# Other tables for the order in which four engines interleave a selective scan with an FFN, on one core

## Chip, cores and metric

The kernel runs on one core of a Trainium2 chip. The metric is the device time in microseconds. A core has four compute engines that run beside one another, each in the order of its own program: TensorE (PE, with its weight loads as PEld), VectorE (DVE), ScalarE (ACT) and GpSimd (POOL). SyncE (SP) issues most of the DMAs. The engines wait for one another only by semaphores.

## What is computed

For a batch of 4 sequences of 256 tokens with 256 features, a mixer and an FFN are added one after the other:

```python
x = x + xattn(ctx, layernorm(x))      # selective scan, gated by silu(layernorm(x))
x = x + ffn(layernorm(x))
# xattn: u = silu(causal_conv4(in_proj(ctx)) + b);  dt_low, B, C = split(x_proj(u))
#        dt = softplus(dt_proj(dt_low) + b);  A = -exp(A_log), 16 states per channel
#        state = state * exp(dt * A) + (dt * u) * B;   y = sum_n state * C + D * u;   out = y * silu(z)
# ffn:   h = layer_norm(gelu(silu(bitlinear(x, w1, b1)))) ;  bitlinear(h, w2, b2)      (256 -> 1024 -> 256)
# bitlinear: rms norm, activations quantised to 8 bits by row, weights to -1, 0, 1 by their mean
```

## The kernel before

**Mixer.** The recurrence over time is done by VectorE's scan instruction. The work is cut into 32 units, `where(k)`: batch b = k // 8, half h of the 256 channels, group of 4 of the 16 states. A unit is 128 channels by 4 x 256 columns. It passes through the engines in this order:

- ScalarE, `exps(k)`: four exponentials give exp(dt * A) into a ring of 6 buffers (L692). It waits for scan k - 6.
- TensorE, `scale_b(k)` and `scale_rest(k)`: 8 small matmuls each (L512) give dt * u * B into one of two PSUM slots. scale_b(k) waits for scan k - 2.
- VectorE, `scan(k)`: L1006, into a ring of 4 buffers. It waits for sum k - 4.
- GpSimd, `prod(k)`: the state times C (L847), for which a DMA has spread C over the partitions.
- TensorE, `sum_states(k)`: 8 transposing matmuls (L551) add the states up in PSUM; a unit that begins a half also adds D * u (L545).

Each batch needs, ahead of its units, small steps: `convolve` (L451), `silu_u` (L658), `xdbl` (L462), `copy_xd` (L664), `dtraw` (L480), `dt_bias` (L672), `dt_neg` (L950), `dt_exp` (L678, L680), `dt_mask` (L955), `dt_series` (L838, L840), `dt_sum` (L966 to L975), `turn_du` (L500) and `copy_du` (L704). Batches 1 to 3 also get blocks with B on their diagonals by way of DRAM (`diagB`, SP's DMAs, L396). The gate of the mixer is `silu_z` (L778), `turn_z` (L567), `copy_z` (L770) and, once a batch's 8 units are summed, `gate` (L1021) and `x1` (L1026), one for each 128 tokens.

**FFN.** Tokens go in 8 tiles of 128, two to a batch. For a batch: `ln1` (L1031 to L1043), `root1` (L854 to L858), `quant1` (L1052 to L1070), `turn_q1` (L577), `copy_q1` (L715), `add_b2` (L864). For a tile t: `bias` (L588), `mm1` (L599), `silu` (L725), `gelu` (L729), `bn2` (L1076, L1080), `root2a` (L872 to L876), `norm` (L735), `gain` (L1094), `shift` (L883), `amax2` (L1101), `square` (L746), `root2b` (L891 to L895), `scales2` (L1109, L1112), `out_scale` (L904, L906), `scale2` (L754), `turn_q2` (L612), `copy_q2` (L761), `mm2` (L619), `res` (L1121) and the store. Tiles 4 to 7 have no norm, shift and scale2; their gain is two VectorE operations (L1086, L1090), and `scale_last` (L911) on GpSimd stands in for scale2. The weights are quantised by `sum_weights`, `wsum`, `wmean`, `scale_weights` and `clip_weights` (L1013, L1015).

**Order.** Each engine runs a loop over k from 0 to 32. In round k it does its part of unit k - 1 (exps, scan, prod or sum_states), and then the steps that its table names for k: `VECTOR_AT`, `SCALAR_AT`, `POOL_AT` and `PE_AT`, written out by hand as strings such as `"gain:1 scales2:0"`. TensorE's scale_b and scale_rest stand in its table too. A step waits by semaphores for its inputs and for the buffers that it overwrites, and all that stands behind it on its engine waits with it. Two regions of PSUM, `head` and `big`, are handed on in the order of TensorE's own list (`take`): turn_z:2 waits for the copy of what held `head` before, bias:4 for that of `big`.

ScalarE holds one set of function tables at a time. Silu and Gelu need sets of their own; Exp and Ln share one. Where a silu or gelu stood in a round, the set with Exp is loaded again (L800) ahead of the next unit's exponentials:

```python
if k:
    if not with_exp:
        nc.scalar.preload_act_table_set("natural_log_exp_and_others")
        with_exp = True
    exps(k - 1)
```

Of the kernel before, what the change touches and what calls it, by code (L numbers as in the profile page):

```python
# [51 lines left out]


VECTOR_AT = (
    "spread_b:1 spread_b:2 dt_half:1",
    "spread_b:3",
    "dt_neg:1",
    "",
    "z_norm:1 dt_mask:1 wmean:0 dt_sum:1",
    "",  # L60
    "dt_neg:2 clip_weights:0",
    "dt_mask:2",
    "",
    "",
    "",
    "gate:0 gate:1 x1:0 x1:1",
    "dt_sum:2 ln1:0",
    "quant1:0 dt_neg:3 clip_weights:1",
    "",
    "",  # L70
    "bn2:0",
    "",
    "gate:2 x1:2 dt_mask:3 dt_sum:3 gain:0 gate:3",
    "x1:3",
    "amax2:0 ln1:1 bn2:1",
    "quant1:1",
    "gain:1 scales2:0",
    "",
    "",
    "amax2:1 bn2:2",  # L80
    "gate:4 gate:5 x1:4 x1:5 gain:2 scales2:1",
    "",
    "res:0 amax2:2 ln1:2 bn2:3 quant1:2",
    "scales2:2",
    "gain:3",
    "",
    "amax2:3 bn2:4 gain:4 gate:6 gate:7 x1:6 x1:7 scales2:3 ln1:3 res:1 quant1:3 bn2:5 amax2:4 gain:5 "
    "scales2:4 res:2 amax2:5 bn2:6 res:3 gain:6 scales2:5 amax2:6 bn2:7 gain:7 scales2:6 res:4 amax2:7 "
    "scales2:7 res:5 res:6 res:7",
)  # L90
SCALAR_AT = (
    "silu_u:1",
    "",
    "copy_xd:1",
    "dt_bias:1 sum_weights:0 dt_exp:1",
    "copy_half:1 sum_weights:1 silu_u:2",
    "copy_xd:2",
    "scale_weights:0 copy_du:1",
    "dt_bias:2",
    "dt_exp:2",  # L100
    "silu_z:0 silu_u:3",
    "copy_z:0",
    "",
    "",
    "",
    "scale_weights:1 copy_xd:3",
    "",
    "copy_du:2",
    "",
    "dt_bias:3",  # L110
    "dt_exp:3 copy_q1:0 silu_z:1 silu:0 silu_z:2 gelu:0 copy_z:1",
    "",
    "",
    "",
    "norm:0",
    "copy_du:3 silu:1 silu_z:3 copy_z:2 square:0 gelu:1",
    "",
    "copy_z:3 norm:1",
    "copy_q1:1",
    "scale2:0 silu:2 square:1 gelu:2 copy_q2:0",  # L120
    "norm:2",
    "",
    "scale2:1 silu:3 square:2 gelu:3",
    "copy_q2:1 norm:3 scale2:2 copy_q1:2 copy_q2:2 silu:4 gelu:4 square:3 silu:5 scale2:3 gelu:5 "
    "copy_q2:3 square:4 copy_q1:3 silu:6 gelu:6 square:5 silu:7 gelu:7 square:6 copy_q2:4 copy_q2:5 "
    "square:7 copy_q2:6 copy_q2:7",
)
POOL_AT = (
    "",
    "",  # L130
    "dt_series:1",
    "z_root:0",
    "",
    "",
    "dt_series:2",
    "",
    "",
    "",
    "",
    "root1:0",  # L140
    "dt_series:3",
    "",
    "",
    "",
    "",
    "root2a:0 shift:0",
    "",
    "root1:1",
    "add_b2:0 root2a:1",
    "root2b:0",  # L150
    "shift:1 out_scale:0",
    "",
    "root2a:2",
    "root2b:1",
    "shift:2",
    "root1:2 root2b:2 root2a:3",
    "",
    "out_scale:1",
    "shift:3",
    "",  # L160
    "root2a:4 root2b:3 out_scale:2 add_b2:1 root1:3 out_scale:3 root2a:5 root2b:4 add_b2:2 scale_last:4 "
    "out_scale:4 root2a:6 root2b:5 scale_last:5 out_scale:5 root2a:7 root2b:6 scale_last:6 root2b:7 "
    "scale_last:7 out_scale:6 add_b2:3 out_scale:7",
)
PE_AT = (
    "scale_b:1 xdbl:1 scale_rest:1 dtraw:1 scale_b:2 convolve:4 scale_rest:2 scale_b:3 turn_half:1 "
    "scale_rest:3 convolve:5",
    "scale_b:4 scale_b:5 wsum:0 scale_rest:4 scale_rest:5 xdbl:2",
    "turn_du:1",
    "convolve:6 scale_b:6 dtraw:2 scale_b:7 scale_rest:6 scale_rest:7",  # L170
    "convolve:7",
    "",
    "turn_z:0 scale_b:8 scale_rest:8 scale_b:9 scale_rest:9",
    "scale_b:10 scale_rest:10 scale_b:11",
    "scale_rest:11 scale_b:12 xdbl:3",
    "",
    "scale_rest:12 turn_du:2 scale_b:13 dtraw:3",
    "scale_rest:13 scale_b:14 turn_q1:0 bias:0 scale_rest:14",
    "mm1:0 turn_z:1 scale_b:15 scale_rest:15",
    "scale_b:16 scale_rest:16",  # L180
    "scale_b:17 scale_rest:17",
    "",
    "bias:1 mm1:1 scale_b:18 turn_du:3 scale_rest:18 scale_b:19 scale_rest:19 turn_z:2 scale_b:20",
    "scale_rest:20 turn_z:3",
    "scale_b:21",
    "",
    "scale_b:22 scale_rest:21 turn_q1:1 bias:2 scale_b:23 scale_rest:22 mm1:2 scale_rest:23",
    "scale_b:24 scale_rest:24 scale_b:25 turn_q2:0 scale_rest:25 scale_b:26",
    "",
    "scale_rest:26",  # L190
    "bias:3 scale_b:27 scale_rest:27 mm1:3 mm2:0",
    "scale_b:28 turn_q2:1 scale_b:29",
    "",
    "scale_rest:28 turn_q1:2 scale_rest:29 scale_b:30",
    "turn_q2:2 scale_b:31 scale_rest:30 bias:4 scale_rest:31 mm1:4",
    "",
    "",
    "bias:5",
    "mm1:5 mm2:1 turn_q2:3 turn_q1:3 bias:6 mm1:6 mm2:2 bias:7 mm2:3 mm1:7 turn_q2:4 turn_q2:5 mm2:4 "
    "turn_q2:6 mm2:5 turn_q2:7 mm2:6 mm2:7",  # L200
)
# [1001 lines left out]
```

## Time and profile before

| | us |
|---|---|
| median of 3 runs | 202.54 |
| lowest and highest | 201.55, 204.31 |
| span of the profiled execution, from its first to its last instruction | 201.9 |
| mean of the runs over that span | 0.6 to 0.9 above it |

The profile describes one execution; its page gives its span, and no device time of its own beside it. A row of instructions gives the time at which the first starts, what they took together, engine, line, operation, what is written and read, how many there are and, in brackets, how long the engine stood idle before them and who released it. The granted clock is 1.0 where TensorE had its full 2.4 GHz and 0.5 at 1.2 GHz.

### The profile page before, as it was taken

What the parts mean: (1) busy time and instruction counts of PE and PEld (TensorE: products, weight loads), DVE (VectorE), ACT (ScalarE), POOL (GpSimd) and SP (SyncE); (2) the same over time, 40 slices, a digit from 0 to 9 for tenths busy, and PEclk for the clock granted to TensorE, in tenths of its full rate; (3) what the DMA queues carried; (4) which work ended last, traced back from release to release, by engine and by line L of the source; (5) the groups of instructions that cost most, each with busy time, mean ns of one, the idle gap of its engine ahead of it and who ended that gap; (6) DMA issues with size and microseconds to landing.
All of it is one profiled execution on the core that took longest, in us unless ns stands there. A gap on an engine that the chain in (4) does not pass through costs nothing.

```text
span 201.9 us, 3382 instructions
## 1 busy us (share of the span) xinstructions
PE 161.6 (80%) x1161; PEld 121.8 (60%) x1167; DVE 164.1 (81%) x249; ACT 161.2 (80%) x262; POOL 142.9 (71%) x139
## 2 busy tenths in 40 slices
...
PEclk9966999999999958999996999999579985995559
...
DMA packets 20193, 20.13 MB, mean 100 GB/s; under 512 B 13448, under 2 KB 16976, under 8 KB 19536
## 3 DMA queue, kind: packets, MB, share of 16 engines
...
## 4 chain that ended last, share of the span: by engine, by line
ACT 24%; PE 24%; POOL 17%; DVE 17%; issue 14%; DMA 1%; DVEq 0%; POOLq 0%; ACTq 0%
ACT dA L692 10%; DVE st L1006 7%; POOL st L847 7%; PE ps L512 4%; PE ps L588 4%; PE ps L451 3%; PE ps L551 3%; DVE stats L1076 3%; PE ps L612 2%; POOL sm L874 2%; PE ps L619 2%; POOL sm L872 2%; ACT w_raw L729 2%; POOL sm L876 1%; PE ps L480 1%
## 5 line engine op out<-in xcount | busy, mean ns | idle before, releaser
L847 POOL TENSOR_TENSOR st<-st,bc 128x1024 f32<-128x1024 f32 x32 | 75.5, 2372 | 19.2 <-DVE st L1006 18.9
L1006 DVE TENSOR_TENSOR_SCAN st<-dA,ps 128x1024 f32<-128x1024 f32 x32 | 72.3, 2276 | 7.5 <-PE ps L512 6.1
L692 ACT ACTIVATE dA<-dt,negA 128x255 f32<-128x255 f32 x128 | 53.2, 498 | 0.2
L512 PE MATMUL ps<-diagB,dtuT 64*128 64x128 f32 x512 | 44.8, 306 | 4.9 <-DVE st L1006 3.5
L512 PEld LDWEIGHTS ps<-diagB,dtuT 64*128 64x128 f32 x512 | 34.9, 198 | 18.1 <-issue 9.5
L551 PE MATMUL ps<-id_f,st 128*128 128x128 f32 x256 | 35.2, 288 | 2.3 <-POOL st L847 2.3
L551 PEld LDWEIGHTS ps<-id_f,st 128*128 128x128 f32 x256 | 29.8, 147 | 5.8 <-POOL st L847 3.0
L612 PE MATMUL ps<-id_f,w_raw 128*128 128x128 f32 x64 | 11.7, 343 | 14.0 <-POOL w_raw L911 8.9
L612 PEld LDWEIGHTS ps<-id_f,w_raw 128*128 128x128 f32 x64 | 9.9, 181 | 15.4 <-issue 13.9
L588 PE MATMUL ps<-rows_sb,diag 128*128 128x512 f32 x32 | 17.2, 663 | 0.4 <-ACT w_raw L725 0.4
L761 ACT ACTIVATE q2T<-ps 128x1024 bf16<-128x1024 f32 x8 | 8.1, 1013 | 10.4 <-PE ps L612 10.4
L725 ACT ACTIVATE w_raw<-ps,sm 128x1024 f32<-128x1024 f32 x8 | 8.9, 1114 | 7.3 <-PE ps L599 7.3
L451 PE MATMUL ps<-ctx_sb,taps_sb 128*128 128x256 f32 (+3 forms) x48 | 13.9, 447 | 0.0
L1076 DVE BATCH_NORM_STATS2 stats<-w_raw 128x6 f32<-128x512 f32 x16 | 10.2, 682 | 2.4 <-ACT w_raw L729 2.4
L451 PEld LDWEIGHTS ps<-ctx_sb,taps_sb 128*128 128x128 f32 x48 | 10.6, 230 | 1.9
L883 POOL TENSOR_TENSOR w_raw<-w_raw,rows_sb 128x1024 f32<-128x1024 f32 x4 | 9.4, 2349 | 2.8 <-DVE w_raw L1094 2.8
L619 PE MATMUL ps<-w2q,q2T 128*128 128x256 bf16 x64 | 10.1, 310 | 0.6 <-DVE res L1121 0.6
L746 ACT ACTIVATE taps_sb<-w_raw 128x1024 bf16<-128x1024 f32 x8 | 8.4, 1049 | 2.7 <-DVE w_raw L1090 1.6
L729 ACT ACT_TABLE_LOAD x8 | 10.3, 1283 | 0.1
L1101 DVE TENSOR_REDUCE am<-w_raw 128x1 f32<-128x1024 f32 x8 | 9.6, 1203 | 0.0
L588 PEld LDWEIGHTS ps<-rows_sb,diag 128*128 128x128 f32 x32 | 6.2, 217 | 5.3 <-issue 5.3
L619 PEld LDWEIGHTS ps<-w2q,q2T 128*128 128x128 bf16 x64 | 7.0, 111 | 3.4 <-DVE res L1121 0.9
...
## 6 DMA issues: line engine op xcount, KB each, us to landing
...
```

The lines of the kernel that those rows point to most:

```text
L451: mm = nc.tensor.matmul(xin(b)[:, h * L + s:(h + 1) * L], inw_taps[:, s, h * P:(h + 1) * P], ctx_sb[:, b * L:(b + 1) * L - s], start=s == ...
L512: mm = nc.tensor.matmul(o[:, i:i + SG // 2, t, r, :], dtuT[rows, b % 2, h, t, :], diagB[rows, b % 2, t, n, :], start=True, stop=True)
L551: mm = nc.tensor.matmul(yT[:, t, h * P:(h + 1) * P], st[:, k % ST_RING, o:o + P], id_f[:, :], is_transpose=True, start=False, stop=h == 1 ...
L588: mm = nc.tensor.matmul(big[:, c], diag[:, t % TPB, :], rows_sb[:, c], start=True, stop=False)
L612: mm = nc.tensor.transpose(o[:, k * P:(k + 1) * P], hid[:, t % HSLOTS, k * P:(k + 1) * P], id_f[:, :])
L619: mm = nc.tensor.matmul(mm2, q2T[:, t % 2, k, :], w2q[:, k, :], start=k == 0, stop=k == KB - 1)
L692: e = nc.scalar.activation(dA[:, k % DA_RING, i * L + 1:(i + 1) * L], dt[:, h, b % 2, 1:L], ACT.Exp, scale=negA[:, h, n:n + 1])
L729: nc.scalar.activation(hid[:, t % HSLOTS], hid[:, t % HSLOTS], ACT.Gelu).then_inc(gelu_done, 1)
L847: tt(s, s, bc[:, ng].rearrange("p s l -> p (s l)"), ALU.mult).then_inc(prod_done, 1)
L1006: nc.vector.tensor_tensor_scan(st[:, k % ST_RING, :], dA[:, k % DA_RING, :], slot(k), 0.0, ALU.mult, ALU.add).then_inc(scanned, 1)
L1076: nc.vector.bn_stats(stats[:, o + i, :], hid[:, t % HSLOTS, 512 * i:512 * (i + 1)]).then_inc(bn2_done, 1)
L1101: nc.vector.tensor_reduce(am2[:, t % 2:t % 2 + 1], hid[:, t % HSLOTS], AX.X, ALU.max, apply_absolute_value=True).then_inc(amax2_done, 1)
```

## The change

The four tables are replaced by others. Every step occurs once, as before; in which round and in what order it stands is new. No operation, buffer or wait is changed. The core of the diff, with the rounds that the prediction speaks of:

```diff
 SCALAR_AT   (round: before | after)
-    4: copy_half:1 sum_weights:1 silu_u:2            9: silu_z:0 silu_u:3
-    19: dt_exp:3 copy_q1:0 silu_z:1 silu:0 silu_z:2 gelu:0 copy_z:1      23: norm:0
-    24: copy_du:3 silu:1 silu_z:3 copy_z:2 square:0 gelu:1               26: copy_z:3 norm:1     27: copy_q1:1
-    28: scale2:0 silu:2 square:1 gelu:2 copy_q2:0    29: norm:2          31: scale2:1 silu:3 square:2 gelu:3
-    32: copy_q2:1 norm:3 scale2:2 copy_q1:2 copy_q2:2 silu:4 gelu:4 square:3 silu:5 scale2:3 gelu:5 ...
+    7: silu_u:2 sum_weights:0 sum_weights:1 copy_xd:2 silu_z:0           15: silu_u:3
+    18: dt_exp:3 copy_q1:0 silu_z:1 silu:0 gelu:0 copy_z:1               21: norm:0
+    24: silu_z:2 square:0 silu_z:3 copy_z:2 silu:1 gelu:1 copy_z:3       26: copy_q1:1 norm:1
+    28: scale2:0 silu:2 gelu:2 copy_q2:0             29, 30, 31: nothing
+    32: square:1 norm:2 silu:3 scale2:1 square:2 copy_q2:1 gelu:3 scale2:2 copy_q1:2 copy_q2:2 norm:3 silu:4 ...
 PE_AT
-    11: scale_rest:13 scale_b:14 turn_q1:0 bias:0 scale_rest:14          12: mm1:0 turn_z:1 scale_b:15 scale_rest:15
-    16: bias:1 mm1:1 ... turn_z:2 scale_b:20    17: scale_rest:20 turn_z:3    24: bias:3 ... mm1:3 mm2:0
-    28: turn_q2:2 scale_b:31 scale_rest:30 bias:4 scale_rest:31 mm1:4    31: bias:5    32: mm1:5 mm2:1 turn_q2:3 ...
-    32 (end): ... turn_q2:4 turn_q2:5 mm2:4 turn_q2:6 mm2:5 turn_q2:7 mm2:6 mm2:7
+    12: dtraw:3 scale_b:14 scale_rest:14 turn_q1:0 bias:0 scale_b:15 mm1:0
+    16: scale_rest:18 scale_rest:19 scale_b:20  18: turn_z:2 scale_rest:20 ... turn_z:3   26: mm1:3
+    29: turn_q2:2 mm2:1     30: bias:4 mm1:4    31: bias:5 mm1:5
+    32 (end): ... turn_q2:4 turn_q2:5 mm2:4 mm2:5 turn_q2:6 mm2:6 turn_q2:7 mm2:7
 POOL_AT
-    25: root2b:1    26: shift:2    27: root1:2 root2b:2 root2a:3    29: out_scale:1    30: shift:3
+    27: root2a:2    28: root2b:1 shift:2 root1:2 root2b:2           30: root2a:3 out_scale:1    31: shift:3
 VECTOR_AT
-    18: gate:2 x1:2 dt_mask:3 dt_sum:3 gain:0 gate:3    26: gate:4 gate:5 x1:4 x1:5 gain:2 scales2:1
-    28: res:0 amax2:2 ln1:2 bn2:3 quant1:2    29: scales2:2     30: gain:3
-    32: amax2:3 bn2:4 gain:4 gate:6 gate:7 x1:6 x1:7 scales2:3 ln1:3 ... amax2:6 bn2:7 gain:7 scales2:6 res:4 ...
+    18: gain:0 gate:2 x1:2 gate:3                       27: gate:4 x1:4 gate:5 x1:5 bn2:2
+    28: res:0 ln1:2 gain:2 scales2:1          30: amax2:2 quant1:2 scales2:2 bn2:3
+    32: gain:3 res:1 amax2:3 bn2:4 gate:6 x1:6 gate:7 x1:7 scales2:3 ln1:3 quant1:3 bn2:5 gain:4 ... bn2:7 amax2:6 gain:7 ...
```

## Rows read from the trace of the kernel before

**Rows 1.** The page: busy time by engine, and the clock in 40 slices of 5.05 us.
```profile
PE 161.6 (80%) x1161; PEld 121.8 (60%) x1167; DVE 164.1 (81%) x249; ACT 161.2 (80%) x262; POOL 142.9 (71%) x139
...
PEclk9966999999999958999996999999579985995559
```
**Rows 2.** The page's costliest groups, the first two: busy, mean ns | idle before, releaser.
```profile
L847 POOL TENSOR_TENSOR st<-st,bc 128x1024 f32<-128x1024 f32 x32 | 75.5, 2372 | 19.2 <-DVE st L1006 18.9
L1006 DVE TENSOR_TENSOR_SCAN st<-dA,ps 128x1024 f32<-128x1024 f32 x32 | 72.3, 2276 | 7.5 <-PE ps L512 6.1
```
**Rows 3.** Windows: stretch, length; busy (count) of PE, PEld, DVE, ACT, POOL; clock, DMA share, GB/s.
```profile
20.00:145.40 125.40, 107.39 (x889) 82.90 (x893) 115.89 (x156) 121.04 (x214) 99.57 (x75) 0.94 0.38 116
145.40:153.10 7.70, 7.54 (x47) 5.46 (x47) 4.87 (x4) 2.31 (x2) 7.51 (x6) 0.80 0.01 2
```
**Rows 4.** Waits of ScalarE from 20 to 146: total, times, longest.
```profile
...
ACT w_raw L725 <- PE ps L599: 1.4, 1, 1.4
ACT taps_sb L746 <- POOL w_raw L883: 1.1, 2, 0.6
ACT w_raw L754 <- DVE sm L1112: 0.7, 1, 0.7
ACT w_raw L735 <- POOL sm L876: 0.3, 1, 0.3
ACT q1T L715 <- PE ps L577: 0.2, 1, 0.2
```
**Rows 5.** ScalarE in order of time: four units' exponentials, unit 31's, copy_q1:2, silu:4.
```profile
87.30 6.48 ACT L692 ACTIVATE dA<-dt,negA 128x255 f32<-128x255 f32 x16
...
138.06 1.28 ACT L800 ACT_TABLE_LOAD   x1
139.36 1.70 ACT L692 ACTIVATE dA<-dt,negA 128x255 f32<-128x255 f32 x4
...
144.81 0.58 ACT L715 ACTIVATE q1T<-ps 128x512 bf16<-128x512 f32 x1
...
153.11 1.11 ACT L725 ACTIVATE w_raw<-ps,sm 128x1024 f32<-128x1024 f32 x1 [2.45 <-PE ps L599]
```
**Rows 6.** The end in order of time, filtered by engine: scale_last:6, turn_q2:7 and res:7.
```profile
190.45 1.12 POOL L911 TENSOR_SCALAR w_raw<-w_raw,sm 128x1024 f32<-128x1024 f32 x1 [0.42 <-DVE sm L1112]
...
195.16 1.59 PE L612 MATMUL ps<-id_f,w_raw 128*128 128x128 f32 x8
...
199.29 0.48 DVE L1121 SCALAR_TENSOR_TENSOR res<-ps,sm,x_nat 128x256 f32<-128x256 f32 x1 [1.14 <-PE ps L619]
```
**Rows 7.** Groups of ScalarE's instructions: the two largest of table loads.
```profile
L729 ACT ACT_TABLE_LOAD x8 | 10.3, 1283 | 0.1
L800 ACT ACT_TABLE_LOAD x7 | 9.0, 1283 | 0.1
```
**Rows 8.** TensorE in order of time, the same steps at both clocks.
```profile
107.06 1.56 PE L551 MATMUL ps<-id_f,st 128*128 128x128 f32 x8 [2.30 <-POOL st L847]
108.55 2.08 PE L512 MATMUL ps<-diagB,dtuT 64*128 64x128 f32 x16
...
117.25 1.50 PE L512 MATMUL ps<-diagB,dtuT 64*128 64x128 f32 x16
...
119.93 1.09 PE L612 MATMUL ps<-id_f,w_raw 128*128 128x128 f32 x8
...
125.58 1.88 PE L588 MATMUL ps<-rows_sb,diag 128*128 128x512 f32 x4
...
146.39 1.91 PE L612 MATMUL ps<-id_f,w_raw 128*128 128x128 f32 x8
...
168.48 3.62 PE L588 MATMUL ps<-rows_sb,diag 128*128 128x512 f32 x4
```
**Rows 9.** GpSimd in order of time: a wait for gain:0, root2a:2 and root2a:4.
```profile
96.25 2.35 POOL L883 TENSOR_TENSOR w_raw<-w_raw,rows_sb 128x1024 f32<-128x1024 f32 x1 [2.83 <-DVE w_raw L1094]
...
124.22 0.21 POOL L872 TENSOR_SCALAR sm<-mv 128x1 f32<-128x1 f32 x1
...
158.25 1.30 POOL L872 TENSOR_SCALAR sm<-mv 128x1 f32<-128x1 f32 x1 [1.29 <-DVE mv L1080]
```

More of the change, by code:

```diff
@@ L54 @@
 VECTOR_AT = (
-    "spread_b:1 spread_b:2 dt_half:1",
+    "spread_b:1 dt_half:1 spread_b:2",
     "spread_b:3",
-    "dt_neg:1",
+    "dt_neg:1 z_norm:1",
+    "dt_mask:1",
     "",
-    "z_norm:1 dt_mask:1 wmean:0 dt_sum:1",
     "",
-    "dt_neg:2 clip_weights:0",
-    "dt_mask:2",
+    "dt_sum:1 wmean:0",
+    "",
+    "clip_weights:0",
+    "dt_neg:2",
+    "gate:0 gate:1 x1:0 x1:1",
+    "ln1:0 dt_mask:2 quant1:0",
+    "dt_sum:2",
+    "clip_weights:1 dt_neg:3",
+    "dt_mask:3",
+    "dt_sum:3",
+    "bn2:0",
+    "",
+    "gain:0 gate:2 x1:2 gate:3",
+    "x1:3 ln1:1",
+    "",
+    "",
+    "bn2:1 quant1:1 amax2:0",
+    "scales2:0 gain:1",
+    "",
+    "",
+    "amax2:1",
+    "gate:4 x1:4 gate:5 x1:5 bn2:2",
+    "res:0 ln1:2 gain:2 scales2:1",
+    "",
+    "amax2:2 quant1:2 scales2:2 bn2:3",
+    "",
+    "gain:3 res:1 amax2:3 bn2:4 gate:6 x1:6 gate:7 x1:7 scales2:3 ln1:3 quant1:3 bn2:5 gain:4 gain:5 res:2 "
+    "amax2:4 amax2:5 scales2:4 bn2:6 res:3 scales2:5 gain:6 bn2:7 amax2:6 gain:7 res:4 scales2:6 amax2:7 res:5 "
+    "scales2:7 res:6 res:7",
+)
+SCALAR_AT = (
+    "silu_u:1",
+    "copy_xd:1",
+    "dt_bias:1",
+    "copy_half:1",
+    "",
+    "dt_exp:1",
+    "",
+    "silu_u:2 sum_weights:0 sum_weights:1 copy_xd:2 silu_z:0",
+    "copy_du:1 scale_weights:0 dt_bias:2",
+    "",
+    "",
+    "copy_z:0",
+    "",
+    "dt_exp:2",
+    "",
+    "silu_u:3",
+    "copy_xd:3 scale_weights:1 copy_du:2",
+    "dt_bias:3",
+    "dt_exp:3 copy_q1:0 silu_z:1 silu:0 gelu:0 copy_z:1",
+    "",
+    "",
+    "norm:0",
+    "",
+    "copy_du:3",
+    "silu_z:2 square:0 silu_z:3 copy_z:2 silu:1 gelu:1 copy_z:3",
+    "",
+    "copy_q1:1 norm:1",
+    "",
+    "scale2:0 silu:2 gelu:2 copy_q2:0",
     "",
@@ L65 @@
     "",
[L66 to L126, printed above, removed]
+    "square:1 norm:2 silu:3 scale2:1 square:2 copy_q2:1 gelu:3 scale2:2 copy_q1:2 copy_q2:2 norm:3 silu:4 "
+    "gelu:4 square:3 silu:5 scale2:3 gelu:5 copy_q2:3 copy_q1:3 silu:6 square:4 gelu:6 square:5 silu:7 gelu:7 "
+    "square:6 copy_q2:4 copy_q2:5 square:7 copy_q2:6 copy_q2:7",
 )
@@ L130 @@
     "",
[L131 to L135, printed above, removed]
+    "z_root:0 dt_series:1",
     "",
@@ L139 @@
     "",
-    "root1:0",
+    "",
+    "",
+    "",
+    "dt_series:2 root1:0",
+    "add_b2:0",
+    "",
     "dt_series:3",
@@ L143 @@
     "",
-    "",
-    "",
[L146 to L151, printed above, removed]
+    "root2a:0",
+    "",
+    "shift:0",
+    "root1:1 root2b:0",
+    "",
+    "root2a:1",
+    "out_scale:0",
+    "shift:1",
+    "",
+    "",
     "",
     "root2a:2",
-    "root2b:1",
-    "shift:2",
-    "root1:2 root2b:2 root2a:3",
+    "root2b:1 shift:2 root1:2 root2b:2",
     "",
-    "out_scale:1",
+    "root2a:3 out_scale:1",
     "shift:3",
-    "",
@@ L161 @@
-    "root2a:4 root2b:3 out_scale:2 add_b2:1 root1:3 out_scale:3 root2a:5 root2b:4 add_b2:2 scale_last:4 "
-    "out_scale:4 root2a:6 root2b:5 scale_last:5 out_scale:5 root2a:7 root2b:6 scale_last:6 root2b:7 "
-    "scale_last:7 out_scale:6 add_b2:3 out_scale:7",
+    "root2b:3 out_scale:2 add_b2:1 root1:3 out_scale:3 root2a:4 add_b2:2 root2a:5 add_b2:3 root2b:4 "
+    "out_scale:4 root2b:5 root2a:6 scale_last:4 out_scale:5 scale_last:5 root2a:7 root2b:6 scale_last:6 "
+    "root2b:7 scale_last:7 out_scale:6 out_scale:7",
@@ L164 @@
 )
 PE_AT = (
-    "scale_b:1 xdbl:1 scale_rest:1 dtraw:1 scale_b:2 convolve:4 scale_rest:2 scale_b:3 turn_half:1 "
-    "scale_rest:3 convolve:5",
-    "scale_b:4 scale_b:5 wsum:0 scale_rest:4 scale_rest:5 xdbl:2",
+    "xdbl:1 scale_b:1 scale_rest:1 dtraw:1 turn_half:1 convolve:4",
+    "scale_b:2 scale_b:3 scale_rest:2 scale_rest:3 convolve:5",
+    "scale_b:4 scale_rest:4 scale_b:5 scale_rest:5 scale_b:6 scale_rest:6 xdbl:2 scale_b:7 scale_rest:7 wsum:0",
     "turn_du:1",
-    "convolve:6 scale_b:6 dtraw:2 scale_b:7 scale_rest:6 scale_rest:7",
@@ L171 @@
-    "convolve:7",
-    "",
-    "turn_z:0 scale_b:8 scale_rest:8 scale_b:9 scale_rest:9",
-    "scale_b:10 scale_rest:10 scale_b:11",
-    "scale_rest:11 scale_b:12 xdbl:3",
-    "",
[L177 to L181, printed above, removed]
-    "",
-    "bias:1 mm1:1 scale_b:18 turn_du:3 scale_rest:18 scale_b:19 scale_rest:19 turn_z:2 scale_b:20",
@@ L184 @@
-    "scale_rest:20 turn_z:3",
-    "scale_b:21",
-    "",
-    "scale_b:22 scale_rest:21 turn_q1:1 bias:2 scale_b:23 scale_rest:22 mm1:2 scale_rest:23",
-    "scale_b:24 scale_rest:24 scale_b:25 turn_q2:0 scale_rest:25 scale_b:26",
-    "",
-    "scale_rest:26",
-    "bias:3 scale_b:27 scale_rest:27 mm1:3 mm2:0",
-    "scale_b:28 turn_q2:1 scale_b:29",
-    "",
-    "scale_rest:28 turn_q1:2 scale_rest:29 scale_b:30",
-    "turn_q2:2 scale_b:31 scale_rest:30 bias:4 scale_rest:31 mm1:4",
-    "",
```

27 lines of the change are left out of this document (23 added, 4 removed).

## The prediction

> **What bounds the kernel now.** I read the busy shares first. All four engines are busy for 71 to 81% of the span [rows 1], so no engine's total explains 201.9 us. The windows split it: from 20 to 145.4 us ScalarE is busy for 121.0 of 125.4 us, and from 145.4 to 153.1 for only 2.3 of 7.7 [rows 3]. ScalarE's waits between 20 and 146 us are next. Without the one before unit 0's exponentials, they come to 3.7 us: 1.4 for mm1:0, 1.1 for shift, 0.7 for scales2:1, 0.3 and 0.2 [rows 4]. So up to 145.4, where copy_q1:2 ends [rows 5], ScalarE's own list is the path, and the other three have slack. Behind it stands a chain across engines: turn_q2:2, rest of the units, bias:4, mm1:4, and silu:4 at 153.11 [rows 5]. From there the last four token tiles run as a chain of dependent steps on all engines, until res:7 starts at 199.29 [rows 6].
>
> **The change, part by part.** All operations stay: 128 exponentials, 32 scans, 32 products and all matmuls. At given durations a table can change only waits, the switches of ScalarE's function tables, which depend on what stands between two units' exponentials, and TensorE's clock. I followed both sets of tables with the durations of the rows: scan 2.28 and product 2.37, each about 0.05 less from start to start [rows 2], exponentials of a unit 6.48/4 = 1.6 [rows 5], taking at each step the later of the engine and what it waits for.
>
> (1) Table loads. Before there are 28: the rows show 8 and 7 at two lines [rows 7], 13 more stand at other lines. After, the same counting gives 27: steps 7, 15, 18, 24 and 28 replace steps 4, 9, 19, 24 and 28 one for one, but silu:3 and gelu:3 leave step 31 for step 32, so that no load brings back the exponential table before unit 31's exponentials. That load lay on ScalarE's path, at 138.06, with the exponentials 1.30 us behind [rows 5]: -1.3 us. The Trainium skill, "ScalarE: Activation LUTs", section "What ACT_TABLE_LOAD costs", puts a drain of about 1.38 us on top of the 1283 ns load. No such time is left between the two starts in these rows; by the page the sum would be 1.4 us lower, still no change that can be told.
>
> (2) ScalarE's waits before 145.4. mm1:0 now directly follows bias:0 and scale_b:15 and ends 1 us before silu:0 asks for it; square:1 and square:2 no longer follow their shift at once; scale2:1 comes after silu:3. In my walk all 3.7 us go. New is a wait of 1.1 us: scale2:2 needs scales2:2, now behind scan 29, amax2:2 (1.2) and quant1:2 (1.7) on VectorE. And norm:3 (1.2 us) goes from before 145.4 to behind copy_q1:2 in ScalarE's list. So copy_q1:2 ends at 145.4 - 1.3 - 3.7 - 1.2 + 1.1 = 140.3 us, if nothing is late.
>
> (3) Behind it. In the new order scale2:2 is followed by turn_q2:2, mm2:1, sum of unit 29, bias:4 and mm1:4. At full clock that is 1.0 + 0.9 + 1.0 + 1.9 + 0.8 = 5.6 us, at half clock about 1.7 + 1.7 + 1.9 + 3.6 + 0.8 = 9.7 (turns 1.09 against 1.91, bias 1.88 against 3.62, [rows 8]). TensorE has an empty stretch just ahead in both orders, and before it ran turn_q2:2 slowly. I take the middle, 7.7, counted from the end of scale2:2 at 139.7: silu:4 at 147.4 (145.3 to 149.4) against 153.1, or -5.7 us.
>
> (4) New thin places. All of (2) is walked at full clock. The most exposed place is units 17 to 19. TensorE's scale_b:20 waits for scan 18, and VectorE does gain:0, gate:2, x1:2 and gate:3 (2.4 us) before that scan, gain:0 itself behind norm:0. I find TensorE without work for 2.8 us there. Before, a gap of 2.30 us was followed by matmuls at half clock: two units' 16 small matmuls in 2.08 us instead of 1.2 to 1.5 [rows 8]. Then come scale_b:20, two sums and turn_z:2, for which silu_z:3 waits on ScalarE with 0.5 us of slack. At half rate these cost 2.5 us more, 2.0 on ScalarE's path; I count +2.0 (0 to 2.5). Semaphore hops and GpSimd's slow instances (1.30 us for a one-column operation that otherwise takes 0.21 [rows 9]) are not in the walk; a wait of 0.2 us at five to ten hops on the path is +1.0 (0 to 3).
>
> (5) The last four tiles. gate:6 to x1:7, ln1:3 and quant1:3 now precede gain:4, and bring bias:6 nearer: -1.1 us by the same walk. At the very end two things cost. amax2:6 (1.2 us) stands between bn2:7 and gain:7; part of it hides root2a:7, and I count +1.1. And mm2:6 now stands before turn_q2:7 on TensorE. Before, turn_q2:7 followed scale_last:7 within a microsecond, at 195.16 [rows 6]. Now turn_q2:6 (1.9 at half clock), copy_q2:6 (1.0) and mm2:6 (0.9 to 1.8) come first, and turn_q2:7 starts about 5 us behind scale_last:6, which ended at 191.57 in the order before [rows 6]: some 1.5 us later than 195.16 (bounds 0.9 and 2.0); +1.5. Together +1.5 (-2 to +3).
>
> Sum: -5.7 + 2.0 + 1.0 + 1.5 = -1.2 us, on a span of 201.9. The median of the runs, 202.54, lies 0.6 us above the span of the profiled execution, and the runs spread from 201.55 to 204.31; I take that execution for a usual one and give 202.5 - 1.2 = 201.3 us.
>
> **DMA.** The blocks and rows of each batch are asked for by counts of products, and these come earlier or as early as before. In the walk diagB for batch 1 is there about 2 us before scale_b:8; the others have 10 us or more. Cost taken: zero; if the first were late, its lateness (up to 2 us) would fall on unit 8, with ScalarE six units ahead.
>
> **Rivals.**
> A. The clock holds. If the two places of (3) and (4) stay at full rate, -2.0 - 2.1 go on top: about 197 us. For it: the order has TensorE's small steps nearer together around steps 20 to 28. Against it: the profile before shows the clock down in 6 stretches, and once behind a gap of 2.30 us [rows 1, 8].
> B. Slower, by one mechanism: GpSimd's step 28. root2b:1, shift:2, root1:2 and root2b:2 stand there ahead of the product of unit 28, and now wait for square:1 and square:2, which moved behind unit 31's exponentials on ScalarE, where silu:3 (for mm1:3, behind sum 25) and scale2:1 (for scales2:1) stand between them. GpSimd runs its list in order, so products 28 to 31 wait for one FFN tile that goes back and forth between three engines. From square:2's end T it takes root2b:2 (1.5), product 28 (2.34) and sum 28 (1.0), then the 7.7 us of (3): silu:4 at T + 12.5. In my walk T is 136.6, which gives 149.1, 1.7 us behind (3) and inside its bounds. Each microsecond that T is later passes on in full; from T = 140.6 silu:4 is as late as now. At T = 143.5 it comes at 156.0, and the end is 202.5 + 2.9 + 1.5 = 207 us. For it: GpSimd waited 2.83 us in one piece for a gain before [rows 9], and here five such hand-overs stand in a row. Against it: the walk has 7 us to spare.
> C. The order is a wash: ScalarE's list is full, what it gains before 145.4 is waited off in front of bias:4, and only the tail's +1.5 remains: 204 us. For it: the 7.7 us behind 145.4 are mostly other engines' [rows 3].
>
> **How the numbers follow.** Forecast 0.47, A 0.27, B 0.13, C 0.13. About 2% (4 us, that is below 198.5 or above 206.6) is what a measurement of this kernel can tell from no change. Nearly all of A and a little of the forecast lie below 198.5: 0.28. B and a little of C lie above: 0.14. The rest, 0.58, is within. The range from 196.0 to 206.0 holds A's centre and C, and leaves out most of B and the far end of A.
>
> **What would show it.** Right: 27 table loads, one fewer at the exponentials' line; ScalarE's waits between 20 and 140 us at 2 to 4 us; copy_q1:2 at 140 to 144 us; a TensorE wait of over 2 us on scan 18, with half-rate matmuls behind; turn_q2:7 behind mm2:6, over 4 us after scale_last:6. Wrong: ScalarE waits of over 6 us before 140 us (a step ordered too early on TensorE, VectorE or GpSimd), a GpSimd wait at root2b that ends after 140 us, with VectorE or TensorE waiting for products behind it (B), or a last scan that ends later than 154.4 us, as it does now. If the last scan comes over 8 us sooner and the end hardly moves, (5) was mis-sized.

## The result, and the profile after

The changed kernel takes 218.64 us (median of 4 runs, 217.85 to 219.51), the kernel before 202.56 us in its runs on the same chip. The ratio is 1.0784 with a 95% interval of 1.0715 to 1.0853: 16 us slower. The forecast was 201.3, with a range up to 206.0 and a chance of 0.14 for slower by over 2%. The profiled execution took 218.56 us, with a span of 216.8. In some kernels executions run over 1.5% longer than the fastest; ratios leave these out, and medians are of all runs.

The page of the kernel after, its lines that answer to [rows 1] and [rows 2] (each line number is one lower than before):

```profile
PE 168.5 (78%) x1161; PEld 125.0 (58%) x1167; DVE 187.6 (87%) x249; ACT 160.7 (74%) x261; POOL 141.8 (65%) x139
...
PEclk9988999967999955799999996999599995995858
...
L846 POOL TENSOR_TENSOR st<-st,bc 128x1024 f32<-128x1024 f32 x32 | 80.2, 2514 | 36.9 <-DVE st L1005 36.6
L1005 DVE TENSOR_TENSOR_SCAN st<-dA,ps 128x1024 f32<-128x1024 f32 x32 | 72.1, 2274 | 2.8 <-PE ps L511 2.3
```

The same 249 instructions keep VectorE busy for 187.6 us instead of 164.1. ScalarE and GpSimd have changed by about a microsecond or less. So no wait between engines explains this first of all: VectorE's instructions themselves became longer. The scans did not (2274 ns against 2276 [rows 2]). The products have 142 ns more each.

Which instructions they are is seen in VectorE's groups, each shape by itself: count, busy us, mean ns. First the kernel before, then the one after.

```profile
L972 DVE SCALAR_TENSOR_TENSOR dt<-sp_v,sp_ln 128x512 f32<-128x512 f32 x3 | 2.1, 693 | 0.1
L1054 DVE TENSOR_TENSOR sm<-amax,sm 128x2 f32<-128x2 f32 x4 | 0.8, 200 | 0.0
L1059 DVE TENSOR_SCALAR sm<-sm,wmean 128x2 f32<-128x2 f32 x4 | 1.0, 242 | 0.0
L1094 DVE TENSOR_TENSOR w_raw<-w_raw,rows_sb 128x1024 f32<-128x1024 f32 x4 | 5.0, 1250 | 0.2 <-ACT w_raw L735 0.2
L1041 DVE TENSOR_SCALAR xc<-x_nat,mv 128x256 f32<-128x256 f32 x8 | 3.1, 429 | 0.0
L975 DVE TENSOR_TENSOR dtu<-dt,cv 128x512 f32<-128x512 f32 x3 | 2.1, 692 | 0.1
L1015 DVE TENSOR_SCALAR w1q<-w_raw 128x2048 bf16<-128x2048 f32 x1 | 1.5, 1536 | 0.0
L1015 DVE TENSOR_SCALAR w2q<-w_raw 128x2048 bf16<-128x2048 f32 x1 | 1.2, 1226 | 0.0
```

```profile
L971 DVE SCALAR_TENSOR_TENSOR dt<-sp_v,sp_ln 128x512 f32<-128x512 f32 x3 | 8.1, 2691 | 0.1
L1093 DVE TENSOR_TENSOR w_raw<-w_raw,rows_sb 128x1024 f32<-128x1024 f32 x4 | 7.4, 1848 | 0.1
L1040 DVE TENSOR_SCALAR xc<-x_nat,mv 128x256 f32<-128x256 f32 x8 | 5.1, 684 | 0.0
L1053 DVE TENSOR_TENSOR sm<-amax,sm 128x2 f32<-128x2 f32 x4 | 4.2, 1051 | 0.1
L974 DVE TENSOR_TENSOR dtu<-dt,cv 128x512 f32<-128x512 f32 x3 | 4.1, 1367 | 0.1
L1058 DVE TENSOR_SCALAR sm<-sm,wmean 128x2 f32<-128x2 f32 x4 | 3.8, 949 | 0.1
L1014 DVE TENSOR_SCALAR w1q<-w_raw 128x2048 bf16<-128x2048 f32 x1 | 3.3, 3267 | 0.0
L1014 DVE TENSOR_SCALAR w2q<-w_raw 128x2048 bf16<-128x2048 f32 x1 | 3.2, 3248 | 0.0
```

In the order of the first list these eight groups grew by 6.0 + 3.4 + 2.8 + 2.4 + 2.0 + 2.0 + 1.8 + 2.0 = 22.4 us; the engine's busy time grew by 23.5. Nothing in them is larger than before; a 128x2 operation takes a microsecond on average. What they have in common is seen in order of time. The kernel after, VectorE and GpSimd in the same stretch, around dt_sum:1 and then quant1:0:

```profile
35.32 10.22 POOL L846 TENSOR_TENSOR st<-st,bc 128x1024 f32<-128x1024 f32 x4
...
40.64 2.69 DVE L971 SCALAR_TENSOR_TENSOR dt<-sp_v,sp_ln 128x512 f32<-128x512 f32 x1
43.37 2.72 DVE L974 TENSOR_TENSOR dtu<-dt,cv 128x512 f32<-128x512 f32 x1
...
66.95 2.34 POOL L846 TENSOR_TENSOR st<-st,bc 128x1024 f32<-128x1024 f32 x1
69.26 1.26 POOL L863 TENSOR_TENSOR x_nat<-x_nat,rows_sb 128x512 f32<-128x512 f32 x1
...
67.02 2.29 DVE L1053 TENSOR_TENSOR sm<-amax,sm 128x2 f32<-128x2 f32 x1
69.42 1.13 DVE L1058 TENSOR_SCALAR sm<-sm,wmean 128x2 f32<-128x2 f32 x1
```

The product runs from 66.95 to 69.29, and an operation on two columns that began at 67.02 ends at 69.31. The next one that is touched, at 69.42, ends with GpSimd's add_b2, at 70.5. And dt and dtu, 0.69 us each when alone, take 2.0 us more each: they began inside the third and the fourth of a row of products, and ran once that one had ended (the fourth at 45.54, dtu at 46.09). In the profile such a standstill counts as busy time, so no view of waits shows it. Now the kernel before, around its dt_sum:2 and quant1:0:

```profile
68.73 0.22 POOL L854 TENSOR_SCALAR sm<-mv 128x2 f32<-128x2 f32 x1 [3.77 <-DVE mv L1036]
...
70.03 2.35 POOL L847 TENSOR_TENSOR st<-st,bc 128x1024 f32<-128x1024 f32 x1
75.80 1.52 POOL L838 TENSOR_SCALAR sp_ser<-sp_e 128x512 f32<-128x512 f32 x1 [3.42 <-ACT sp_e L678]
...
66.34 0.69 DVE L972 SCALAR_TENSOR_TENSOR dt<-sp_v,sp_ln 128x512 f32<-128x512 f32 x1
67.07 0.69 DVE L975 TENSOR_TENSOR dtu<-dt,cv 128x512 f32<-128x512 f32 x1
...
72.04 0.36 DVE L1054 TENSOR_TENSOR sm<-amax,sm 128x2 f32<-128x2 f32 x1
```

There GpSimd's table has root1:0 and dt_series:3 in front of a product, and both wait. While they wait (3.77 and 3.42 us), VectorE does dt_sum:2, quant1:0, dt_neg:3 and the clipping of w2 at full speed. The order before kept the two engines apart by waits that looked like idle time of an engine with slack.

What it does to the rest, in the windows from 20 to 98 us, before and then after (stretch, length; busy and count of PE, PEld, DVE, ACT, POOL; clock, DMA):

```profile
20.00:98.00 78.00, 68.74 (x567) 52.88 (x568) 71.18 (x87) 75.99 (x148) 54.62 (x34) 0.96 0.48 144
```

```profile
20.00:98.00 78.00, 65.22 (x488) 50.21 (x488) 76.14 (x77) 63.19 (x121) 51.01 (x30) 0.87 0.43 139
```

ScalarE was the full engine, with 75.99 of 78 us. Now it is VectorE, with 76.14, and it gets 77 instructions done in place of 87. ScalarE's waits from 20 to 170 us in the kernel after, in answer to [rows 4] (total, times, longest):

```profile
ACT dtuT L703 <- PE ps L499: 7.9, 2, 5.3
ACT w_raw L753 <- DVE sm L1111: 5.3, 2, 4.2
ACT sp_v L671 <- PE ps L479: 4.6, 2, 3.0
ACT q2T L760 <- PE ps L611: 3.8, 2, 3.1
```

With three smaller ones they come to 26.2 us, 24.3 of them up to the end of copy_q1:2 (162.9 us). Up to the same step it was 3.7 us before. The start of scan 15 slips from 82.92 to 94.43 us, and the end of the last scan from 154.45 to 167.0. The remaining 2.3 of the 14.8 us between the two starts of res:7 (199.29 [rows 6] and 214.12) come behind the last scan.

The Trainium skill, "SBUF — State Buffer", section "SBUF: two separate sides", has a rule for this: VectorE and GpSimd share a pair of ports by "an exclusive lock, not a bandwidth split", and whoever starts first has it for the whole instruction. On VectorE it concerns fast modes and operations with two inputs in SBUF, the latter only against a GpSimd operation that reads SBUF. The rows above agree: a 2.34 us product, a 2.29 us standstill of 128x2. So do the scans, whose second input is in PSUM.

### The profile page after: what moved, and what is told of

Same layout as the page of the kernel before. It is cut to its first block and busy times, and to the rows that moved or that the text cites. A ratio compares the mean times of both kernels' runs of the same rounds, so it can differ in the third digit from the quotient of the medians.

```text
span 216.8 us, 3381 instructions
## 1 busy us (share of the span) xinstructions
PE 168.5 (78%) x1161; PEld 125.0 (58%) x1167; DVE 187.6 (87%) x249; ACT 160.7 (74%) x261; POOL 141.8 (65%) x139
## 3 DMA queue, kind: packets, MB, share of 16 engines
HBM read 17.70 MB, written 2.21 MB: 92 GB/s over the span
## 5 line engine op out<-in xcount | busy, mean ns | idle before, releaser
L846 POOL TENSOR_TENSOR st<-st,bc 128x1024 f32<-128x1024 f32 x32 | 80.2, 2514 | 36.9 <-DVE st L1005 36.6
L1005 DVE TENSOR_TENSOR_SCAN st<-dA,ps 128x1024 f32<-128x1024 f32 x32 | 72.1, 2274 | 2.8 <-PE ps L511 2.3
L550 PE MATMUL ps<-id_f,st 128*128 128x128 f32 x256 | 37.2, 298 | 0.7 <-POOL st L846 0.7
L550 PEld LDWEIGHTS ps<-id_f,st 128*128 128x128 f32 x256 | 32.4, 155 | 3.3 <-POOL st L846 1.2
L611 PE MATMUL ps<-id_f,w_raw 128*128 128x128 f32 x64 | 13.2, 376 | 13.7 <-POOL w_raw L910 7.4
L611 PEld LDWEIGHTS ps<-id_f,w_raw 128*128 128x128 f32 x64 | 10.8, 195 | 15.6 <-issue 15.4
L587 PE MATMUL ps<-rows_sb,diag 128*128 128x512 f32 x32 | 19.0, 724 | 0.8 <-ACT w_raw L724 0.8
L450 PE MATMUL ps<-ctx_sb,taps_sb 128*128 128x256 f32 (+3 forms) x48 | 13.2, 429 | 0.0
L450 PEld LDWEIGHTS ps<-ctx_sb,taps_sb 128*128 128x128 f32 x48 | 9.9, 214 | 1.8
L1120 DVE SCALAR_TENSOR_TENSOR res<-ps,sm,x_nat 128x256 f32<-128x256 f32 x8 | 3.8, 476 | 7.2 <-PE ps L618 7.2
```

Source lines behind the costliest of these rows:

```text
L450: mm = nc.tensor.matmul(xin(b)[:, h * L + s:(h + 1) * L], inw_taps[:, s, h * P:(h + 1) * P], ctx_sb[:, b * L:(b + 1) * L - s], start=s == ...
L550: mm = nc.tensor.matmul(yT[:, t, h * P:(h + 1) * P], st[:, k % ST_RING, o:o + P], id_f[:, :], is_transpose=True, start=False, stop=h == 1 ...
L587: mm = nc.tensor.matmul(big[:, c], diag[:, t % TPB, :], rows_sb[:, c], start=True, stop=False)
L611: mm = nc.tensor.transpose(o[:, k * P:(k + 1) * P], hid[:, t % HSLOTS, k * P:(k + 1) * P], id_f[:, :])
L846: tt(s, s, bc[:, ng].rearrange("p s l -> p (s l)"), ALU.mult).then_inc(prod_done, 1)
L1005: nc.vector.tensor_tensor_scan(st[:, k % ST_RING, :], dA[:, k % DA_RING, :], slot(k), 0.0, ALU.mult, ALU.add).then_inc(scanned, 1)
```

## Experiments

Theory 1: the time is what VectorE stands still beside GpSimd's products. Theory 2: the new order itself puts steps too early or too late, and the longer operations hang beside that. The first three experiments add waits only; the next two take the products' work away in either order. An edit that adds lines shifts the line numbers behind it.

**1. Three products held back until dt_sum is done.** The edit, in the kernel after:

```diff
+            holds = {5: (dt_step, 9), 11: (dt_step, 12), 14: (dt_step, 15)}
...
+                if k in holds:
+                    pool.wait_ge(*holds[k])
```

> The changed kernel, with three more waits on GpSimd: the products of units 5, 11 and 14 start only when VectorE's dt_sum of the same round is done (2.1 us without a hindrance, but 6.5, 4.1 and 4.1 us in the changed kernel). Theory 1 (VectorE's operations that read SBUF twice stand still while a product of GpSimd runs): dt_sum takes 2.1 to 3 us each time, VectorE's busy time falls by 5 to 8 us, and the kernel gets faster by 3 to 7 us, though only waits were added: 212 to 216 us. Theory 2 (the loss comes from the order in which TensorE and ScalarE wait for each other): more waits can't help, 218 to 222 us.

Measured: 220.53 us; one run took 216.43 and three 220.49 to 220.94, too far apart for a ratio. The profile is of the run with 216.43. Its VectorE groups, and the place of the first hold:

```profile
L1097 DVE TENSOR_TENSOR w_raw<-w_raw,rows_sb 128x1024 f32<-128x1024 f32 x4 | 9.3, 2333 | 0.4 <-ACT w_raw L734 0.4
L975 DVE SCALAR_TENSOR_TENSOR dt<-sp_v,sp_ln 128x512 f32<-128x512 f32 x3 | 4.1, 1360 | 0.1
```

```profile
45.62 2.20 DVE L1142 TENSOR_SCALAR wmean<-wmean 128x2 f32<-128x2 f32 x1
...
45.45 2.35 POOL L850 TENSOR_TENSOR st<-st,bc 128x1024 f32<-128x1024 f32 x1 [1.35 <-DVE dtu L978]
```

dtu came free as meant (4.1 to 2.1 us) and dt in two of three places (8.1 to 4.1; the one at 41.95 us still took 2.69). But the product that was released by dtu at once stopped the next sensitive operation, a mean of 128x2, for 2.20 us, and gain rose from 7.4 to 9.3. A few holds displace the standstill: VectorE is busy for 186.3 us, 1.3 less, where theory 1 had 5 to 8 less. That was a miss for theory 1's numbers. The time decides nothing: the three longer runs lie where theory 2 had them, the fastest just above theory 1's range.

**2. Ten products held back**, at every place where I had seen a collision.

```diff
+            holds = {5: (dt_step, 9), 7: (w_clip, 2), 10: (diag_done, 2), 11: (dt_step, 12), 12: (w_clip, 4), 14: (dt_step, 15), 18: (xc_done, 4), 22: (gained, 2), 27: (xc_done, 6), 29: (diag_done, 6)}
```

> As hold_dtsums, with ten such waits: the products of units 5, 7, 10, 11, 12, 14, 18, 22, 27 and 29 each wait until the steps of VectorE's round (dt_sum, clip_weights, ln1 and quant1, gain:1) are done. Theory 1: of the 23.8 us by which VectorE is busier than in the kernel before, 15 or more go, and the time falls to 205 to 213 us; the rest is the price of products that start 2 to 4 us late. Theory 2: not faster than 218 us, rather 220 to 226.

Measured: 209.09 us, 1.0212 of the kernel before (1.0129 to 1.0295), so less than the changed kernel by waits alone: by 9.6 us in the medians, and by 11.6 us by the two ratios. The busy time of VectorE is 172.8 us, 14.8 less, where 15 were expected. Its groups:

```profile
L975 DVE SCALAR_TENSOR_TENSOR dt<-sp_v,sp_ln 128x512 f32<-128x512 f32 x3 | 3.0, 1001 | 0.1
L1018 DVE TENSOR_SCALAR w1q<-w_raw 128x2048 bf16<-128x2048 f32 x1 | 1.2, 1227 | 0.0
```

By theory 2 more waits can only cost; they gave back 10 to 12 of 16 us.

**3. The first six of these holds** (5 to 14).

> The changed kernel with the first six of the ten waits of hold_all: the products of units 5, 7, 10, 11, 12 and 14. Theory 1: most of the standstill lies before 95 us (15 of 23.8 us), so these six bring the larger part: 210 to 214 us, with VectorE 10 to 13 us less busy than in the changed kernel. If the gain of hold_all came from its later four: 215 us or more.

Measured: 215.87 us (211.56 to 217.61); the spread is too wide for a ratio. VectorE is busy for 180.8 us, 6.8 less than in the changed kernel, where 10 to 13 were expected. Again gain (9.3 us) and others took what dt gave up. So the late places count too, and how much each is worth by itself stays open.

**4. The products cut to 8 of their 1024 columns**, once in the order after, once in the order before. The rest of the product with C is left out.

```diff
-                tt(s, s, bc[:, ng].rearrange("p s l -> p (s l)"), ALU.mult).then_inc(prod_done, 1)
+                tt(s[:, 0:8], s[:, 0:8], bc[:, ng].rearrange("p s l -> p (s l)")[:, 0:8], ALU.mult).then_inc(prod_done, 1)
```

> The changed kernel with each of GpSimd's 32 products cut to 8 of its 1024 columns (the multiplication by C is left out for the rest). Theory 1: VectorE's busy time falls from 187.6 to about 165 us, and the time to 190 to 203 us. Theory 2: VectorE's busy time falls too, but the changed kernel stays over 10 us above the kernel before with the same cut.

> The kernel before with the same cut of the products to 8 columns (the multiplication by C is left out for the rest). Theory 1: VectorE stays near 163 us, the time falls only a little, to 195 to 202 us, and the distance to the changed kernel with the same cut is under 4 us instead of 16. Theory 2: the distance stays at over 10 us.

Measured: 198.24 us in the order after, ratio 0.9815 (0.9746 to 0.9884), and 200.35 in the order before, 0.9873 (0.9791 to 0.9955). By the medians the products cost the order after 20.4 us and the order before 2.2; by the ratios it is 19.6 and 2.6. Without them the new order is 2.1 us ahead by the medians and 1.2 by the ratios, whose intervals overlap, so that a lead isn't shown; the walk of the prediction, which knew no collisions, had it ahead by 1.2. VectorE is busy for 165.2 and 163.0 us. Of the 16 us nothing is left for theory 2 to explain. This pair alone doesn't separate a lock from the mere length of the products, since both go. The next pair keeps the length.

**5. Products replaced by fills of the same length**, in either order: 8 columns of the product and two fills of a spare tile, which write SBUF and read nothing.

```diff
+                tt(s[:, 0:8], s[:, 0:8], bc[:, ng].rearrange("p s l -> p (s l)")[:, 0:8], ALU.mult)
+                for j in range(2):
+                    if k or j:
+                        pool.wait_ge(padded, 2 * k + j)
+                    last = nc.gpsimd.memset(pad[:, :], 0.0)
+                    last.then_inc(padded, 1)
+                pool.wait_ge(padded, 2 * (k + 1))
+                nc.gpsimd.memset(mark[:, k:k + 1], 0.0).then_inc(prod_done, 1)
```

> The changed kernel, where each product of GpSimd is cut to 8 of 1024 columns (the rest of the multiplication by C is left out) and followed by fills of a spare buffer of 2500 columns, which read nothing: GpSimd is busy with each unit for about 2.4 to 2.8 us, as long as with the product, and sum_states still waits for the end of it. Theory 1 in its narrow form (VectorE stands still only while GpSimd reads SBUF for a product): VectorE's dt, dtu and the small quant1 operations keep their undisturbed 0.69 and 0.15 us, and the kernel takes 198 to 204 us. Theory 3 (it is GpSimd's lateness that the cut took away, not the standstill of VectorE): 214 to 220 us.

> The kernel before with the same replacement of the products (the same part of the multiplication by C is left out). Theory 1: 200 to 205 us, within 3 us of the changed kernel with the replacement. Theory 3: as far from it as the two kernels are, 12 to 16 us below.

Measured: order after 206.61 us, ratio 0.9976 (0.9899 to 1.0053); order before 205.45, ratio 1.014 (1.0101 to 1.0179). The eight runs of the first spread from 201.00 to 210.95 us, so I read no order between the two. Both medians lie above what theory 1 expected (198 to 204, 200 to 205), and far below theory 3's 214 to 220. GpSimd is at least as busy as in the changed kernel (149.4 against 141.8 us), and 12 of the 16 us are gone by the medians, all of them by the ratios. The length of GpSimd's work is not the cause. The trace of the order after:

```profile
64.35 0.16 DVE L1063 TENSOR_TENSOR sm<-amax,sm 128x2 f32<-128x2 f32 x1
...
64.62 0.97 DVE L1068 TENSOR_SCALAR sm<-sm,wmean 128x2 f32<-128x2 f32 x1
64.75 2.18 DVE L1071 TENSOR_SCALAR xc<-xc,sm 128x256 f32<-128x256 f32 x2
...
64.42 2.37 POOL L853 MEMSET pad<- 128x1250 f32 x2
```

dt and dtu are back at 692 ns each. Operations with one SBUF tensor as input still stand still, now until the end of one fill (1.17 us) and not of a product: xc from 0.60 to 2.18. The narrow form of theory 1 didn't have this; VectorE is busy for 172.5 us here and for 164.8 in the order before.

**6. The kernel before without two of its covers**: on GpSimd root1:0 goes from round 11 to 12, behind a product, and dt_series:3 from 12 to 16.

```diff
-    "root1:0",
-    "dt_series:3",
...
+    "root1:0",
...
+    "dt_series:3",
```

> The kernel before with two entries of GpSimd's table moved back: root1:0 from round 11 to 12 and dt_series:3 from round 12 to 16, so that the products of units 10, 11 and 12 no longer stand behind waits for VectorE's ln1:0 and ScalarE's dt_exp:3. Theory 1: these waits kept GpSimd off while VectorE did dt_sum:2, quant1:0 and clip_weights:1; without them VectorE's dt, dtu, sm or w2q operations take 2 to 3 us somewhere in 63 to 80 us, VectorE is 3 to 8 us busier, and the kernel is 1 to 6 us slower though its products start earlier: 203.5 to 209 us. Theory 2 (waits only cost): the same or faster, 200 to 202.5 us.

Measured: 206.97 us, ratio 1.0216 (1.0147 to 1.0286), some 4 us slower, with VectorE 3.7 us busier, both within what theory 1 expected. GpSimd's waits ahead of root1 and dt_series fell from 9.0 to 3.9 us; those for scans rose from 18.9 to 25.7. Its trace:

```profile
64.93 2.69 DVE L972 SCALAR_TENSOR_TENSOR dt<-sp_v,sp_ln 128x512 f32<-128x512 f32 x1
72.87 2.31 DVE L1059 TENSOR_SCALAR sm<-sm,wmean 128x2 f32<-128x2 f32 x1
...
64.39 2.67 POOL L847 TENSOR_TENSOR st<-st,bc 128x1024 f32<-128x1024 f32 x1 [0.84 <-DVE st L1006]
72.80 2.36 POOL L847 TENSOR_TENSOR st<-st,bc 128x1024 f32<-128x1024 f32 x1 [2.15 <-DVE st L1006]
```

The same collisions, made in the fast kernel by moving two small GpSimd steps. This is the plainest evidence for theory 1. Both steps also come later than before; what that costs by itself wasn't separated.

**7. The tail's matmul order undone**, in the kernel after: turn_q2:7 ahead of mm2:6 again.

```diff
-    "turn_q2:7 mm2:7",
+    "turn_q2:7 mm2:6 mm2:7",
```

(mm2:6 is taken out of the line above it.)

> The changed kernel with the end of TensorE's table as it was before: turn_q2:7 ahead of mm2:6 again. Step (5) of the prediction: turn_q2:7 starts 1 to 1.5 us earlier against scale_last:6 than the 4.8 us of the changed kernel, and the time falls by 1 to 1.5 us, to 217 to 217.7 us. If TensorE's clock or VectorE's res:5 decide there instead, within 0.5 us of the changed kernel.

Measured: 219.36 us, ratio 1.0808 (1.0758 to 1.0859), no gain. From the end of scale_last:7 to the start of res:7 it takes 6.26 us, in the changed kernel 6.24 (207.88 to 214.12), in the kernel before 4.97 (194.32 to 199.29). So the tail's end is 1.3 us longer than before, but undoing this one swap doesn't give it back. turn_q2:7 does start 0.15 us behind scale_last:7's end instead of 2.05. Then mm2:6 (1.91 us) and res:6 stand in front of mm2:7, and mm2:7 runs at half clock, in 1.85 us instead of 1.03.

**8. One table load less in the kernel before**: step (1) alone. ScalarE's silu:3, square:2 and gelu:3 go from round 31 to 32.

```diff
-    "scale2:1 silu:3 square:2 gelu:3",
-    "copy_q2:1 norm:3 scale2:2 copy_q1:2 copy_q2:2 silu:4 gelu:4 square:3 silu:5 scale2:3 gelu:5 "
+    "scale2:1",
+    "silu:3 square:2 gelu:3 copy_q2:1 norm:3 scale2:2 copy_q1:2 copy_q2:2 silu:4 gelu:4 square:3 silu:5 scale2:3 gelu:5 "
```

> The kernel before with silu:3, square:2 and gelu:3 moved from the end of ScalarE's round 31 to the start of round 32, behind unit 31's exponentials: one load of the function tables less. If step (1) of the prediction holds alone: 27 loads, the exponentials of unit 31 some 7 us earlier, silu:3 1.6 us later, and 1.3 us less in all, 200.5 to 202 us; if the stretch behind 145.4 us is set by TensorE and VectorE, nothing measurable, 202 to 203 us.

Measured: 200.18 us, ratio 0.9859 (0.9799 to 0.9918): 1.4% less than before, under the 2% of the forecast's bound, but the whole interval lies below 1; the median is 0.3 us below the range expected. The mean granted clock of the runs behind the ratio is 0.91 to 0.93, in the kernel before 0.89 to 0.91. Its ScalarE at unit 31 and at silu:4, where [rows 5] has 139.36 and 153.11:

```profile
129.90 1.69 ACT L692 ACTIVATE dA<-dt,negA 128x255 f32<-128x255 f32 x4
...
150.25 1.12 ACT L725 ACTIVATE w_raw<-ps,sm 128x1024 f32<-128x1024 f32 x1 [2.45 <-PE ps L599]
```

It is faster than both kernels.

**9. The same with mm2:5 ahead of turn_q2:6** on TensorE.

> The kernel before_one_load_less with one more step moved: mm2:5 ahead of turn_q2:6 on TensorE, where it falls into the wait for scale_last:6. By the rows turn_q2:7 then follows scale_last:7 at once instead of waiting for mm2:5 (0.8 us): 199.4 to 200.2 us, faster than the kernel before by 1.2 to 1.6%. If mm2:5 delays turn_q2:6 by as much: 200.2 to 201 us.

Measured: 202.32 us (198.86 to 203.71), ratio 0.9834 (0.9768 to 0.99), with its kernel before at 203.92; the median lies above both ranges expected. The interval overlaps that of experiment 8, so no further gain can be told. The profile shows the same as in experiment 7: turn_q2:7 starts 2.9 us behind the end of scale_last:6 instead of 3.6, but it and mm2:6 take 1.94 and 1.91 us, at half clock, where experiment 8 has 1.04 each, and res:7 comes 8.2 us behind instead of 7.2.

A kernel that swaps one engine's whole table and keeps the others wasn't tried.

## Why the prediction was wrong

**The premise failed, not a term of the sum.** "At given durations a table can change only waits, the switches of ScalarE's function tables … and TensorE's clock": durations were taken as given. They depend on what GpSimd does at that moment. The order chooses that, and it is worth 17 to 18 us here (19.6 less 2.6 by the ratios, 20.4 less 2.2 by the medians, experiment 4). I walked both tables with the undisturbed means and so walked past 22 us of VectorE's time. The rows that could have warned me were there: [rows 2]'s product had 18.9 us of idle time ahead of it, which I read as slack, and [rows 9]'s wait of 2.83 us was the cover under which gain:0 ran.

**(1) One table load fewer**: right. The kernel after has 261 instructions on ScalarE instead of 262. Put alone into the order before, the edit gave 2.9 us (0.0141 of 202.6, between 1.7 and 4.1) where I had 1.3. It also moves silu:3, square:2 and gelu:3 behind unit 31's exponentials. What of it is the load, the move and the higher clock wasn't separated.

**(2) ScalarE's waits**: forecast 1.1 us new with all 3.7 gone; there are 24.3 us up to the end of copy_q1:2. Two of the largest, 7.9 us for turn_du and 5.3 for scales2, are behind VectorE steps that stood still. With small products they are 4.9 us, of which 1.2 are the wait for turn_z:2 that step (4) had priced. So without collisions the waits are 4.9 us against 4.1 in the forecast (1.1, and the 3.0 of step (4)). copy_q1:2 ends at 162.9 in the kernel after and at 142.8 with small products; the forecast was 140.3, or 143.3 with step (4).

**(3) silu:4**: forecast 147.4 (145.3 to 149.4), and 150.4 with the 3.0 us of step (4). Measured: 168.24, and 148.91 with small products. The stretch from scale2:2's end on was sized well: 7.7 us counted, 7.3 there, and 5.8 in the kernel after. But the order before has silu:4 at 149.44 with small products, 3.7 earlier than with whole ones. So the new order gains 0.5 us at this point and not 2.7; part of the 153.11 that I set out from was itself the products'.

**(4) Clock and thin places**: TensorE's gap ahead of scale_b:20 came as walked, 2.42 us for 2.8. In the kernel after no half clock stood behind it; with small products it did, behind a gap of 2.96 us. First the kernel after:

```profile
107.80 0.71 PE L511 MATMUL ps<-diagB,dtuT 64*128 64x128 f32 x8 [2.42 <-DVE st L1005]
...
108.99 1.91 PE L550 MATMUL ps<-id_f,st 128*128 128x128 f32 x16
```

```profile
94.64 0.72 PE L511 MATMUL ps<-diagB,dtuT 64*128 64x128 f32 x8 [2.96 <-DVE st L1005]
95.29 1.20 PE L544 MATMUL ps<-diag_D,cv 128*128 128x128 f32 x4
96.28 3.13 PE L550 MATMUL ps<-id_f,st 128*128 128x128 f32 x16
```

Sixteen transposes in 1.91 us are the fast figure; [rows 8] has 16 small matmuls in 2.08 behind 2.30 us. The slow transposes with small products made silu_z:3 wait 1.2 us for turn_z:2, on ScalarE's path, where I had +2.0. With ten holds (experiment 2) the gap is 2.42 us again, and the same 16 transposes take 3.02. So the mechanism of +2.0 is real and was sized somewhat high, but behind a gap of 2.42 us both clocks are seen; what decides stays open. The clock did fall elsewhere, to 0.87 over 20 to 98 us (0.96 before), where VectorE was the full engine; what that cost by itself wasn't measured.

**(5) The tail**: +1.5 forecast, of which mm2:6 ahead of turn_q2:7 was to be +1.5. In the kernel after turn_q2:7 starts 4.8 us behind the end of scale_last:6 (about 5 forecast, 3.6 before), and res:7 9.0 behind it (7.7 before). So this place was walked rightly, but experiment 7 gained nothing by undoing the swap. The tail as a whole was mis-sized. With small products the time from silu:4 to res:7 is 43.55 us in the order after (148.91 to 192.46) and 45.60 before (149.44 to 195.04). The new tail is 2.0 us better, not 1.5 worse. How much of that is the clock (last four slices of the page 5978 after, 5559 before, with small products) stays open. Between these two traces the new order is 2.6 us ahead, where the walk had 1.2. That it was so near is luck: its gain at silu:4 was too large by 2.2, and its tail too bad by 3.5.

**The rivals.** None named the mechanism. A (the clock holds) and C (a wash) fall with the premise. B had the right sign and some of the place: GpSimd's product 28 waited behind root2b:2 until 155.12 and fell on VectorE's quant1:2, two of whose 128x2 operations took 1.61 and 2.21 us. From the start of scan 28 to that of scan 30 it is 12.3 us, against 8.4 before. But scan 28 was 9.2 us late by then, which B doesn't know. My own sign for a wrong forecast, ScalarE waits of over 6 us before 140, came up (18.0 us), and so did a last scan that ends after 154.4 (167.0); my reading of the first, "a step ordered too early", wasn't the cause. **The DMAs** cost nothing, as said. One point of scale: the runs are 1.76 us above the span in the kernel after, and 1.76 to 1.87 in the experiments, so the profiled execution before was nearer to 203.7 than to the median; that is a microsecond of the forecast, and small beside the rest.
